# An attention kernel's transfer order, the turning of its input rows, a split weighing, and reciprocals stored by tile

## What is computed

```python
q = jnp.einsum('bim,mhd->bhid', x, wq)      # 8 heads of 128
k = jnp.einsum('bim,mhd->bhid', x, wk)
v = jnp.einsum('bim,mhd->bhid', x, wv)
q = rope(q)                                 # halves exchanged, times sin, plus times cos
k = rope(k)
s = jnp.einsum('bhid,bhjd->bhij', q, k) / 128
s = s - 1e30 * (i < j)                      # causal
p = jax.nn.softmax(s, axis=-1)
o = jnp.einsum('bhij,bhjd->bhid', p, v)
return jnp.einsum('bhid,hdm->bim', o, wo)
```

## Time and profile before

| | |
|---|---|
| median of 3 runs | 1963.05 us (1960.64 to 1964.24) |
| profiled execution | 1951.72 us, span 1949.9 us |
| mean granted TensorE clock | 0.973 |
| busy: PE, DVE, ACT, POOL | 1777.2, 1577.5, 1240.9, 1081.5 us |

### The profile page before, as it was taken

How to read it: one execution, slowest core, us unless ns; L and a number is a source line. 1 busy time by engine, 2 the same in 40 slices (tenths; PEclk the granted TensorE clock), 3 DMA queues, 4 the chain that set the end, 5 groups by cost and what they waited for, 6 DMA issues and landing times. The chain is left out here.

```text
span 1949.9 us, 33601 instructions
## 1 busy us (share of the span) xinstructions
PE 1777.2 (91%) x10556; PEld 1527.5 (78%) x10556; DVE 1577.5 (81%) x2926; ACT 1240.9 (64%) x2450; POOL 1081.5 (55%) x661
## 2 busy tenths in 40 slices
PE   4899989998999899989998999899999949999997
PEld 4788877887788778867887888688888837878886
DVE  3879987997899778978997789788889856777674
ACT  2767766776777667756776677577767615445553
POOL 3556655664666556555665556566656433455543
PEclk7999999999999999999999999999999979999999
DMA  3322232223222322232223222322233120111100
GB/s 105 80 60 82 66 87 57 75 66 89 66 66 66 87 66 66 66 89 66 66 66 87 66 66 66 87 66 66 74 82 82 48 81 22 46 42 32 35 19 22
DMA packets 69767, 127.90 MB, mean 66 GB/s; under 512 B 15456, under 2 KB 42080, under 8 KB 69600
## 3 DMA queue, kind: packets, MB, share of 16 engines
q1 hardware_dynamic: 68416, 124.81, 23.5%
q10 hardware_dynamic: 1184, 1.05, 0.2%
HBM read 50.07 MB, written 8.65 MB: 30 GB/s over the span
## 5 line engine op out<-in xcount | busy, mean ns | idle before, releaser
L448 ACT ACTIVATE probs<-ps_slot,neg_max 128x640 f32<-128x640 f32 (+7 forms) x512 | 379.1, 742 | 172.7 <-DVE neg_max L533 165.2
L533 DVE CUSTOM_DVE_ANT_0 ps_slot<-ps_slot,causal 128x640 f32<-128x640 f32 (+7 forms) x512 | 385.5, 753 | 39.5 <-PE ps_slot L57 38.5
L681 PE MATMUL ps_turn<-ident,probs 128*128 128x128 f32 x2304 | 339.0, 278 | 54.6 <-DVE pt_high L564 34.7
L681 PEld LDWEIGHTS ps_turn<-ident,probs 128*128 128x128 f32 x2304 | 264.9, 142 | 95.3 <-DVE pt_high L564 37.9
L55 PE MATMUL ps_slot<-k,q 128*128 128x512 f32 (+3 forms) x768 | 284.1, 370 | 39.3 <-DVE rot_q L549 38.6
L412 POOL TENSOR_TENSOR q<-rot_q,q 128x1024 fp32r<-128x1024 f32 x64 | 154.0, 2406 | 269.9 <-ACT q L465 269.9
L56 PE MATMUL ps_slot<-k,q 128*128 128x512 f32 (+3 forms) x768 | 267.3, 348 | 0.0
L57 PE MATMUL ps_slot<-k,q 128*128 128x512 f32 (+3 forms) x768 | 267.0, 348 | 0.0
L412 POOL TENSOR_TENSOR k<-rot_k,k 128x1024 fp32r<-128x1024 f32 x64 | 153.0, 2390 | 112.0 <-ACT k L465 111.8
L556 DVE TENSOR_TENSOR rot_k<-rot_k,swapped_k 128x1024 f32<-128x1024 f32 x64 | 177.8, 2779 | 35.8 <-POOL swapped_k L404 35.8
L55 PEld LDWEIGHTS ps_slot<-k,q 128*128 128x128 f32 x768 | 145.9, 190 | 69.9 <-DVE rot_q L549 53.5
(11 more groups left out here) (165 smaller groups left out, 4551.8 us busy)
## 6 DMA issues: line engine op xcount, KB each, us to landing
swapped_k<-unrot_k SPq DMA_DIRECT2D x128, 256.0 KB, 3.6
swapped_q<-unrot_q SPq DMA_DIRECT2D x128, 256.0 KB, 3.7
inv_b<-inv_rows SPq DMA_DIRECT2D x64, 512.0 KB, 4.7
x_rows<-in_L_attn_x SPq DMA_DIRECT2D x8, 512.0 KB, 5.3
y_t<-y_sum SPq DMA_DIRECT2D x8, 512.0 KB, 3.4
y_in<-y_t SPq DMA_DIRECT2D x7, 512.0 KB, 3.7
x_row<-in_L_attn_x SPq DMA_DIRECT2D x7, 512.0 KB, 4.9
out<-out_row SPq DMA_DIRECT2D x7, 512.0 KB, 3.2
```

The lines of the kernel that those rows point to most:

```text
L448: act.activation(probs_tile(t), score_tile(name, head, i), ACT.Exp, scale=-1.0, bias=neg_max[:, head.par, t:t + 1], accum_out=sums[:, head ...
L533: dve.tensor_tensor_reduce(tile, tile, causal[:, T - WIDTH[t]:T], -1.0, UNSEEN, ALU.add, ALU.min, neg_max[:, head.par, t:t + 1]).then_inc( ...
L681: last = pe.transpose(bank[:, at:at + P], probs_tile(t)[:, j * P:(j + 1) * P], ident[:, :])
```

## The change

It has five parts.

- `store_inv` writes the reciprocals tile by tile, so that each of the 1024 values goes to its own place in DRAM (pieces of 4 bytes, before 128 pieces of 32 bytes), and `scale_y` reads `inv_b` without a step.
- SP's step becomes `swap` k, `store_inv`, `swap` q, `store_y` of the head two back (one step later than before), `load_x_rows`, `spread_inv`. SP runs one step more at the end.
- `turn_x` is called for one half at the end of the step as before, and for the other half in the next step between `project_v` and the scores s32; the wait for `x_lo` moves behind these scores, and the fill 5b of that step with it. ScalarE and VectorE follow.
- `weigh_high` is split: its first two of four tiles stay ahead of the projections, the last two (256 and 128 columns) come behind them.
- In the step after `turn_x`, VectorE does `split_v_lo` and the second half of x ahead of the row maximum of s32.

The diff, cut to its core:

```diff
 (SP)
-                sp.dma_start(inv_rows[head.par, :].rearrange("(p t) -> p t", t=NT), inv[:, head.par, :])\
+                sp.dma_start(inv_rows[head.par, :].rearrange("(t p) -> p t", p=P), inv[:, head.par, :],
+                             allow_slow_non_contiguous=True)\
                   .then_inc(inv_stored, 16)
...
                 swap(0, after)
-                spread_inv(before)
-                store_y(before)
+                store_y(head.step(-2))
                 if loads_x(head.step(2)):
                     load_x_rows(head.step(2).batch() + 1)
-
-            steps(sp, step, 16)
+                spread_inv(before)
+
+            steps(sp, step, 17)
 (ScalarE)
                 split_v_hi(before)
+                if loads_x(before):
+                    split_x_hi(before, 1)
                 split_hi(0, head)
+                if loads_x(before):
+                    turn("5b", before)
...
                 turn("6a", head, split_done)
-                split_x_hi(head)
-                turn("5b", head)
+                if loads_x(head):
+                    split_x_hi(head, 0)
+                else:
+                    turn("5b", head)
 (VectorE)
-                tiles = slice(4 * g, 4 * g + 4)
-                dve.tensor_tensor(y_head[:, g * BANK:(g + 1) * BANK].rearrange("d (t p) -> d t p", p=P),
-                                  ps_y[:, g, :].rearrange("d (t p) -> d t p", p=P),
-                                  inv_b[:, :].rearrange("d (p t) -> d t p", t=NT)[:, tiles, :],
-                                  ALU.mult).then_inc(y_scaled[g], 1)
+                cols = slice(g * BANK, (g + 1) * BANK)
+                dve.tensor_tensor(y_head[:, cols], ps_y[:, g, :], inv_b[:, cols], ALU.mult).then_inc(y_scaled[g], 1)
...
                 turn("6a", head)
-                split_x_lo(head)
-                turn("5b", head)
+                if loads_x(head):
+                    split_x_lo(head, 0)
+                else:
+                    turn("5b", head)
                 scale_y(1, before)
-                rowmax("s32", head, 1)
-                split_v_lo(head)
+                if loads_x(head):
+                    split_v_lo(head)
+                    split_x_lo(head, 1)
+                    rowmax("s32", head, 1)
+                    turn("5b", head)
+                else:
+                    rowmax("s32", head, 1)
+                    split_v_lo(head)
                 rowmax("s32", head, 0)
 (TensorE)
-            def turn_x(head):
-                if not loads_x(head):
-                    return
+            def turn_x(head, half):
                 pe.wait_ge(x_rows_landed, head.batch() * 16 + 16)
-                for half, bank_of in enumerate(("6b", "6a")):
-                    pe.wait_ge(turn_lo, head.turns(bank_of))
-                    for t in range(4 * half, 4 * half + 4):
...
+                pe.wait_ge(turn_lo, head.turns(("6b", "6a")[half]))
+                for t in range(4 * half, 4 * half + 4):
...
                 before, after = head.step(-1), head.step(1)
-                if loads_x(before):
-                    pe.wait_ge(x_lo, before.batch() * 2 + 2)
-                turn("5b", before, ("6b", before))
+                if not loads_x(before):
+                    turn("5b", before, ("6b", before))
...
                     pe.wait_ge(lo_made[0], before.made())
+                if loads_x(before):
+                    turn_x(before, 1)
                 scores("s32", before)
-                turn("4a", before, ("6a", before))
+                if loads_x(before):
+                    pe.wait_ge(x_lo, before.batch() * 2 + 1)
+                    turn("5b", before)
+                    pe.wait_ge(x_lo, before.batch() * 2 + 2)
+                    turn("4a", before)
+                else:
+                    turn("4a", before, ("6a", before))
                 turn("7a", before, ("5b", before))
-                weigh_high(before)
+                weigh_high(before, (0, 1))
                 free_slot(v_lo, before, -2, -2, 2)
                 project(1, after)
                 free_slot(exped[3], before)
                 project(0, after)
+                weigh_high(before, (2, 3))
                 turn("2", before, ("4a", before))
...
                 turn("6a", head, ("7b", head))
-                turn_x(head)
+                if loads_x(head):
+                    turn_x(head, 0)
```

More of the change, by code:

```diff
@@ L326, in loads_x, with x_bank, x_half @@
             return head.no == X_STEP and head.live() and (not isinstance(head.loop, int) or head.batch() + 1 < B)
+        def x_bank(head, half):
+            return ps_turn[:, (head.at + 1 + half) % 2, :]
+        def x_half(head, half, part):
+            return kept.x_t[(head.at // 8 + 1) % 2][:, part, half * BANK:(half + 1) * BANK]
         block = ctx.enter_context(nc.Block())
@@ L483, in turn, with split_x_hi @@
                 last.then_inc(turn_hi, 1)
-            def split_x_hi(head):
-                if not loads_x(head):
-                    return
-                x_next = kept.x_t[(head.at // 8 + 1) % 2]
-                for half in range(2):
-                    act.wait_ge(x_turned, head.batch() * 2 + (half + 1))
-                    act.activation(x_next[:, 0, half * BANK:(half + 1) * BANK],
-                                   ps_turn[:, (head.at + 11 + half) % 2, :], ACT.Copy).then_inc(x_hi, 1)
+            def split_x_hi(head, half):
+                act.wait_ge(x_turned, head.batch() * 2 + (half + 1))
+                act.activation(x_half(head, half, 0), x_bank(head, half), ACT.Copy).then_inc(x_hi, 1)
             def step(head):
@@ L683, in turn, with weigh @@
                 last.then_inc(turned, 1)
-            def turn_x(head):
-                if not loads_x(head):
-                    return
+            def turn_x(head, half):
                 pe.wait_ge(x_rows_landed, head.batch() * 16 + 16)
-                for half, bank_of in enumerate(("6b", "6a")):
-                    pe.wait_ge(turn_lo, head.turns(bank_of))
-                    for t in range(4 * half, 4 * half + 4):
-                        last = pe.transpose(ps_turn[:, (head.at + 11 + half) % 2, t % 4 * P:(t % 4 + 1) * P],
-                                            kept.x_rows[:, t, :], ident[:, :])
-                    last.then_inc(x_turned, 1)
-            def weigh(head, out, probs_t, j_first, start, stop, done):
-                for j in range(4):
+                pe.wait_ge(turn_lo, head.turns(("6b", "6a")[half]))
+                for t in range(4 * half, 4 * half + 4):
+                    last = pe.transpose(x_bank(head, half)[:, t % 4 * P:(t % 4 + 1) * P], kept.x_rows[:, t, :],
+                                        ident[:, :])
+                last.then_inc(x_turned, 1)
+            def weigh(head, out, probs_t, j_first, start, stop, js=range(4)):
+                for j in js:
                     c0 = j * P if probs_t is not pt_split else 0
@@ L703, in weigh, with weigh_high @@
                                         start and j == 0, stop and j == 3)
-                last.then_inc(done, 1)
-            def weigh_high(head):
+                return last
+            def weigh_high(head, js):
                 if not head.live():
                     return
-                pe.wait_ge(turn_lo, head.turns("5b"))
-                if head.step(-1).live():
-                    pe.wait_ge(y_scaled[1], head.step(-1).made())
-                weigh(head, ps_y[:, 1, :], pt_high, 4, True, False, high_done)
+                if 0 in js:
+                    pe.wait_ge(turn_lo, head.turns("5b"))
+                    if head.step(-1).live():
+                        pe.wait_ge(y_scaled[1], head.step(-1).made())
+                last = weigh(head, ps_y[:, 1, :], pt_high, 4, True, False, js)
+                if 3 in js:
+                    last.then_inc(high_done, 1)
             def weigh_split(head):
@@ L717, in weigh_split @@
                 pe.wait_ge(turn_lo, head.turns("5a"))
-                weigh(head, ps_y[:, 1, :], pt_split, 0, False, True, split_done)
+                weigh(head, ps_y[:, 1, :], pt_split, 0, False, True).then_inc(split_done, 1)
             def weigh_low(head):
```

15 lines of the change are left out of this document (5 added, 10 removed).

## The result

The changed kernel takes **2110.49 us** (median of 4 runs, 2103.76 to 2114.11), the one before 1963.64 (1960.64 to 1965.4): a ratio of 1.0743, 95% interval 1.0724 to 1.0762. It is 147 us slower where 106 us of gain were forecast. The third rival is what happened, in its main lines. The profiled execution has a span of 2112.3 us.

A forecast was written before the change was run, and what follows sets the result against it. TensorE was taken as near its end, losing time to a wait every step, long steps and 14 disturbed steps. Gains 27.5 + 16 + 49 + 14 - 1, say 106 us, from 1963.05 gave 1857 us; range 1836 to 1890.

The forecast's parts named there:

- The third rival: Store of 1024 pieces holds SP's queue, delaying `swapped_q` behind it; kernel slower, 2080 us at 6 us delay; chance 0.05.
- The store by tile: Reciprocals' store on SP's queue: 1024 pieces cost 1.9 us more (bounds 0 and 13.3), landing `swapped_q` later; 16 us gained.
- The weighing split: Matmuls moved behind the projections fill TensorE's wait for L549: 0.45 of 0.60 us in 61 steps, 27.5 us gained.
- Long steps against short: Whether GpSimd's sines of q start before VectorE's addition for k makes 32 steps 0.5 us longer: 16 us to gain.
- `scale_y`: VectorE's scaling read without a step falls from 1143 to 681 ns, 59 us of VectorE, counted as nothing by itself.
- The big transfers: Rows load and sum store moved behind `swapped_q` on SP's queue make seven batch-end steps short: 49 us gained, bounds 35 and 49.
- The turning of rows: Turning x in two places shortens TensorE's waits in seven steps, to 25.95 us each: 14 us gained, bounds 0 and 33.

The follow-up runs named there:

- e12: Changed kernel storing 512 pieces of 8 bytes, plus ten lone stores of 4-byte pieces at varied counts and distances behind its last step: 2047.99 us; only store durations count.
- e1: Changed kernel with the reciprocals stored row by row and read with a step of 32 bytes, as before the change: 1875.81 us, 0.9562 of the kernel before.
- e11: Changed kernel with reciprocals stored by row, and GpSimd beginning the sines of q only after VectorE's addition for k: 1852.1 us, 0.9434 of the kernel before.
- e13: Kernel before with one wait alone: GpSimd begins the sines of q only after VectorE's addition for k: 1924.77 us, ratio 0.9808.
- e3: Changed kernel storing the reciprocals in pairs (512 pieces of 8 bytes), scale_y reading with a step of two values: 1866.02 us, 0.9506 of the kernel before.
- e10: Changed kernel storing pairs (512 pieces of 8 bytes), and GpSimd beginning the sines of q only after VectorE's addition for k: 1856.45 us, 0.9456 of the kernel before.

## Why the prediction was wrong

**The step that failed** is in "The store by tile": "I take 1.9, since the rows load has as many pieces and bigger ones." The bounds, 0 and 13.3 us, did hold the truth: the store got 7.8 us longer (10.0 against 2.2) and the sines of q start 5.6 us later in the median. The choice between them went by the wrong likeness. The rows load has as many pieces, but they are big and go into SBUF, not into neighbouring places of DRAM; e12 shows that the number of pieces hardly matters and the distance at which they end does. No row of the kernel before showed a write of that sort, so the far end deserved far more than the 5% it got. The Trainium skill's rule on strided last dimensions ("DMA: Bandwidth & Descriptors", "Rules for kernel authors") spoke against exactly this store. The trace bears it out as to the count, with 57,344 more packets, and as to the advice. The rule gives no time, and the count is not what sets the price here: 1024 pieces of 32 bytes took 1.8 us.

**The mechanism of the third rival was right in its place** (`swapped_q` directly behind the store), and wrong in one link: it had VectorE's addition for k late, which starts 6.4 us into the step before and after (medians); late is the addition for q, 14.5 us into it instead of 12.4. By its working a delay of 5.6 us gives 3.25 a step, 201 in 62 steps, 2058 us. Measured are 2110, and not all of it is waiting. Against e1, over the same 63 steps, TensorE stands 164 us more (201.5 against 37.7), and the same matmuls take 67 us more, nearly all of it in the 41 steps with a granted clock below 1.00. The prediction had priced a falling clock in the steps with the turning; the rival left it out. The addition for q, now beside another instruction of GpSimd, takes 3.29 us in the median instead of 2.12 and is part of the waiting; its share was not measured.

**The other terms.**
- *The weighing split*: 27.5 put in, 19 measured alone. The wait of TensorE went, and the short steps gained the 0.45 us worked out, to 21.70. The size was off because a long step gained only 0.25 (what holds it was not traced), and the batch ends gave 5.6 us back. The two terms were not independent: with the order set as well (e11) 44 of the 47 ordinary steps are 21.7 to 21.9.
- *Long steps against short*: right that the order of GpSimd and VectorE makes them, and right that a later start on GpSimd is free. It is worth 36 us alone (e13) and 25 on top of the other parts (0.9562 to 0.9434 of 1961), not 16: the ordinary steps do give 16 in the profile, the disturbed ones some 11 more. (The prediction counted 46 ordinary steps, 32 of them long; there are 47 and 33.) That a slow transfer should bring it about was the mistake; a wait brings it at no cost.
- *`scale_y`*: 1143 to 676 ns as forecast, and rightly counted at nothing by itself. Pairs gain 10 us over rows (e1, e3), and nothing once the order is set (e11, e10).
- *The big transfers*: 49 forecast, 48 measured.
- *The turning of rows*: 14 forecast, 22 measured. The step comes near what was worked out, 25.6 us against 25.95, but in part by luck: 1.0 us of the sum was for a falling clock, which did not fall, so the other terms are 0.65 us short. The seven gain 16.5 us; what the medians show beyond that no stretch of the profile explains.

In the changed kernel itself little of this could be seen. The additions for k, the vanished wait for L549 and `scale_y` came as forecast. The batch ends can't be told from the other steps either, but they average 25.9 us, because nearly every step is that long.

The forecast of 1857 us was there to be had, with 1852: by the three other parts of this change and a wait in place of the fourth. That the total comes so near the forecast is in part luck, since the misses of the terms go both ways.

## What to carry to other kernels

Before a transposing store of single values goes to DRAM, ask how close together the separate writes end, not how many there are: by themselves, 4 bytes apart, they took 9 to 10.5 us, in pairs 4.2, as rows of 32 bytes 1.1. Count the clock with the wait: between e1 and the changed kernel, 164 us more of standing went with 67 us more for the same matmuls. Take the stride on the reading side, where a step of 8 bytes cost VectorE nothing. If an order between two engines pays, set it with a wait, and not by making a transfer late. And when the two ends of an unknown price lie on two sides of the break-even, give the bad side a chance of that size, and not 5% because a comfortable row lies near.

## What the runs showed of the hardware that was not expected

- Single 4-byte writes to neighbouring places in DRAM are slow even with no other transfer of the attention beside them: 128 of them take nearly as long as 1024 (9.1 and 10.5 us), and 1024 of them 64 bytes apart take 2.5 us. About 0.6 us for each write of a 64-byte stretch is an estimate from these times, and the length of the stretch is open.
- The exchange of q, two transfers of 256 KB each, issued from 0.54 us behind such a store on, was seen as arrived only when the store had landed, although the store moves 4 KB. Whether its bytes or only the sign of their landing came late was not measured.
- In the step shown, TensorE's granted clock is 0.50 (1.2 GHz) in the stretch behind a wait of 3.24 us, and 1.00 again from 148 on. In the step from 201.73 to 225.68 TensorE stands for 1.73 us in all, and the clock is 1.00 throughout.
- VectorE's product with a second operand of stride 8 bytes takes 679 ns, as without a stride; at 16 bytes 1068, at 32 bytes 1144.
- A wait of 2.1 us a step (120.8 us in 58), added to GpSimd in the kernel before, made the kernel 1.9% faster, since it keeps GpSimd off VectorE's addition: 1.22 us alone, up to 3.4 beside it.
